# Last batch's attention product in split float16, with all engine orders rewritten

## The reference, cut to what matters

```python
def _xattn(teacher_logits, teacher_features, Wq, bq, Wk, bk):
    query = einsum('bnc,dc->bnd', teacher_features, Wq) + bq      # features: (4, 512, 256), d = 128
    key = einsum('bnc,dc->bnd', teacher_features, Wk) + bk
    attention = softmax(einsum('bnd,bmd->bnm', query, key), axis=-1)
    return einsum('bln,bmn->blm', teacher_logits, attention)      # (4, 512, 512)

x = x + _xattn(layernorm(x), ctx_1024, Wq, bq, Wk, bk)            # x: (4, 512, 512)
x = x + _ffn(layernorm(x), gate_w, up_w, down_w)
```

## Time and profile before

| | us |
|---|---|
| median of 3 runs | 609.17 |
| lowest, highest | 608.98, 626.26 |
| the profiled execution's own time | 610.21 |
| its span in the profile | 608.4 |
| TensorE busy in the span | 596.0 (98%) |
| VectorE busy | 484.3 (80%) |
| ScalarE busy | 316.6 (52%) |

### The profile page before, as it was taken

How to read it: one execution, slowest core, us unless ns; L and a number is a source line. 1 busy time by engine, 2 the same in 40 slices (tenths; PEclk the granted TensorE clock), 3 DMA queues, 4 the chain that set the end, 5 groups by cost and what they waited for, 6 DMA issues and landing times.

```text
span 608.4 us, 7111 instructions
## 1 busy us (share of the span) xinstructions
PE 596.0 (98%) x2619; PEld 274.1 (45%) x2619; DVE 484.3 (80%) x455; ACT 316.6 (52%) x466; POOL 54.4 (9%) x60
## 2 busy tenths in 40 slices
PE   8998999999999899999999999999999999999998
PEld 3444444444444344444444444444444444444446
DVE  4999879997998998879848598857499699575850
ACT  3999999955444425355735436554031522432441
POOL 0020101310200301001000111010000000000010
PEclk9998999999999999999999999999999999999999
DMA  8968789979677408957786788956432105755393
GB/s 319 392 142 247 234 177 295 229 176 287 136 218 170 112 2 258 219 132 178 193 144 129 160 201 222 172 121 122 86 67 40 17 1 86 106 102 87 70 164 62
DMA packets 148212, 95.43 MB, mean 157 GB/s; under 512 B 134353, under 2 KB 134737, under 8 KB 142801
## 3 DMA queue, kind: packets, MB, share of 16 engines
q1 hardware_dynamic: 142704, 66.92, 46.4%
q0 software_dynamic: 5472, 28.05, 20.1%
HBM read 26.81 MB, written 10.49 MB: 61 GB/s over the span
## 4 chain that ended last, share of the span: by engine, by line
PE 63%; DVE 11%; DMA 10%; ACT 8%; issue 7%; SPq 1%; DVEq 0%; ACTq 0%; POOLq 0%
PE bank L759 26%; PE bank L771 17%; PE bank L774 9%; PE bank L743 5%; DMA W<-hT 3%; PE bank L720 2%; DMA h<-hT 2%; PE bank L728 2%; ACT mag L958 2%; DMA gu_lo<-hT 1%; PE bank L789 1%; DVE h L1680 1%; DVE h L1692 1%; DVE h L1496 1%; DVE hscale L1675 1%
## 5 line engine op out<-in xcount | busy, mean ns | idle before, releaser
L759 PE MATMUL bank<-gu_hi,xT 128*128 128x512 f16 x1024 | 245.1, 379 | 3.9 <-ACT silu L1126 3.8
L759 PEld LDWEIGHTS bank<-gu_hi,xT 128*128 128x128 f16 x1024 | 99.4, 98 | 127.0 <-issue 6.1
L759 PE MATMUL bank<-gu_lo,xT 128*128 128x512 f16 x512 | 131.4, 379 | 0.0
L771 PE MATMUL bank<-dn,hT 128*128 128x512 f16 x480 | 106.1, 379 | 1.2 <-ACT silu L1126 1.2
L1126 ACT ACTIVATE silu<-bank,unscale 128x512 f32<-128x512 f32 x64 | 43.0, 679 | 75.3 <-PE bank L759 34.7
L759 PEld LDWEIGHTS bank<-gu_lo,xT 128*128 128x128 f16 x512 | 50.1, 98 | 60.4
L1663 DVE SCALAR_TENSOR_TENSOR h<-bank,unscale,silu 128x512 f32<-128x512 f32 x64 | 47.1, 747 | 34.4 <-ACT silu L1126 19.4
L771 PEld LDWEIGHTS bank<-dn,hT 128*128 128x128 f16 x480 | 46.9, 98 | 58.1 <-ACT silu L1126 1.7
L1496 DVE SCALAR_TENSOR_TENSOR h<-mag,h 128x2048 f32<-128x2048 bf16 x18 | 41.2, 2289 | 32.0 <-ACT mag L958 32.0
L743 PE MATMUL bank<-dn,h 128*128 128x512 f32 x128 | 57.8, 607 | 1.9 <-ACT dn L1043 1.9
L958 ACT ACTIVATE mag<-h 128x2048 bf16<-128x2048 f32 x18 | 34.3, 1905 | 40.0 <-DVE h L1680 30.5
(11 more groups left out here) (134 smaller groups left out, 569.9 us busy)
## 6 DMA issues: line engine op xcount, KB each, us to landing
W<-hT POOLq DMA_DIRECT2D x12, 1024.0 KB, 6.0
W<-in_units SPq DMA_DIRECT2D x11, 1024.0 KB, 5.8
h<-W POOLq DMA_DIRECT2D x7, 1024.0 KB, 5.9
h<-in_xcols SPq DMA_DIRECT2D x4, 1024.0 KB, 11.1
out_y<-y POOLq DMA_DIRECT2D x12, 256.0 KB, 4.5
h<-in_xrows SPq DMA_DIRECT2D x2, 1024.0 KB, 12.6
h<-hT POOLq DMA_DIRECT2D x2, 1024.0 KB, 6.2
out_y<-h SPq DMA_DIRECT2D x2, 1024.0 KB, 5.1
```

What stands on the lines that cost most here:

```text
L759: last = pe.matmul(bank[:, :], xT[:, b % 2, part, k, :], w[:, c, g, j * 512:(j + 1) * 512], start=(j == 0 and not low), stop=(j == HT - 1 ...
L771: pe.matmul(bank[:, :], hT[:, r % 2, 0, k, :], dn[:, w, k, :], start=(k == 0 and w == 0), stop=False)
```

## The change

For the batches in `split`, which is batch 3 alone, `attend` is done with float16 factors. x is multiplied by one scale `xup` for the whole batch, found from the largest of (mean squared plus sum of squares) over the rows: `bound` on VectorE, an all-reduce over the partitions on GpSimd (`bound_max`), a logarithm and an exponential on ScalarE (`x_scale`). The scaled x is split in two float16 parts, `xt_hi` on ScalarE and `xt_lo` on VectorE; the turned probabilities, times 2^14, are split by `take_probs` on ScalarE and `probs_lo` on VectorE. Each tile then has twelve float16 matmuls in place of four float32 ones. `x_unscale` makes the factor with which `add_attended` takes the scales out again. `center` of batch 2 now also waits for the attended tiles of all batches, since the parts of x lie where it writes.

```diff
 def attend(b, lt):
-    for j in range(HT):
-        last = pe.matmul(bank[:, :], xTf[b % 2][:, j, lt * P:(lt + 1) * P], AT[:, j, :],
-                         start=(j == 0), stop=(j == HT - 1))
+    if b in split:
+        pe.wait_ge(xlo_ready, split.index(b) + 1)
+        for n, (p, q) in enumerate(((0, 0), (0, 1), (1, 0))):
+            for j in range(HT):
+                last = pe.matmul(bank[:, :], xT_parts[b][:, p, j, lt * P:(lt + 1) * P], AT_parts[:, q, j, :],
+                                 start=(n == 0 and j == 0), stop=(n == 2 and j == HT - 1))
...
+def xt_hi(b):                        # ScalarE
+    act.wait_ge(xdown_ready, n + 1)
+    act.wait_ge(probs_turned, LT * (4 - b))
+    nc.scalar.activation(xT_parts[b][:, 0, :, :], xTf[b % 2], ACT.Copy, scale=xup[:, n:n + 1])
...
+def xt_lo(b):                        # VectorE
+    dve.wait_ge(xhi_ready, n + 1)
+    dve.scalar_tensor_tensor(xT_parts[b][:, 1, :, :], xTf[b % 2], xup[:, n:n + 1], xT_parts[b][:, 0, :, :],
+                             ALU.mult, ALU.subtract)
...
+def probs_lo(b, nt):                 # VectorE
+    dve.scalar_tensor_tensor(AT_parts[:, 1, :, cols], bank_of(f"t{b}.{nt}"), A_SCALE,
+                             AT_parts[:, 0, :, cols], ALU.mult, ALU.subtract)
...
 TensorE's order, from the last tile of batch 2 on
             attend(2, 3)
+            product(2, 0)
+            product(1, 0)
             turn_probs(3, 0)
+            product(3, 0)
             turn_probs(3, 1)
+            product(0, 0)
             turn_probs(3, 2)
-            product(3, 0)
-            product(1, 0)
-            product(2, 0)
+            product(0, 1)
             turn_probs(3, 3)
-            product(0, 0)
+            product(3, 1)
+            product(2, 1)
             attend(3, 0)
             attend(3, 1)
             attend(3, 2)
+            attend(3, 3)
             product(1, 1)
-            product(3, 1)
-            attend(3, 3)
-            product(0, 1)
-            product(2, 1)
...
 SyncE's order, the first loads
+            load_consts()
             load_slice(0)
             load_ctx(0)
-            load_consts()
+            load_rows(0)
             load_half(0)
             load_rest(0)
```

More of the change, by code:

```diff
@@ L89, in xattn_ffn @@
     slice_size = 256
+    split = (3,)
     parked = (5, 6)
@@ L238, in xattn_ffn @@
         xmean_ready = sem("xmean_ready")
-        xstats_ready = [sem(f"xstats{b}_ready") for b in range(B)]
         ymean_ready = sem("ymean_ready")
@@ L741, in attend @@
                 pe.wait_ge(at_ready, LT * (b + 1))
-                for j in range(HT):
-                    last = pe.matmul(bank[:, :], xTf[b % 2][:, j, lt * P:(lt + 1) * P], AT[:, j, :],
-                                     start=(j == 0), stop=(j == HT - 1))
+                if b in split:
[4 more added lines that the diff above has]
+                                             start=(n == 0 and j == 0), stop=(n == 2 and j == HT - 1))
+                else:
+                    for j in range(HT):
+                        last = pe.matmul(bank[:, :], xTf[b % 2][:, j, lt * P:(lt + 1) * P], AT[:, j, :],
+                                         start=(j == 0), stop=(j == HT - 1))
                 last.then_inc(attended, 1)
@@ L1541, in add_attended @@
                 row = slice(LT * b + lt, LT * b + lt + 1)
[L1542 removed]
+                if b in split:
+                    dve.wait_ge(xatt_ready, split.index(b) + 1)
+                each = xatt if b in split else xrstd
+                dve.scalar_tensor_tensor(rows, bank_of(f"a{b}.{lt}")[:, :], each[:, row], rows, ALU.mult, ALU.add,
                                          accum_out=ysum[:, row]).then_inc(x1_ready, 1)
@@ L1824, in _ @@
+            unit_reduce(8)
+            rows_round(2)
+            rows_dequant(2)
+            unit_largest(8)
+            hidden_of(5, 2)
             hidden_of(6, 2)
+            unit_scale(8)
+            hidden_of(0, 2)
             unit_reduce(9)
-            unit_largest(8)
+            attended_means(3)
+            hidden_of(2, 2)
+            unit_power(8)
+            unit_round(8)
+            unit_reduce(10)
+            hidden_of(4, 2)
             hidden_of(3, 2)
+            unit_dequant(8)
@@ new lines, in _ @@
+            hidden_scale(9)
+            hidden_dequant(8)
+            hidden_lo(7)
+            hidden_of(12, 1)
+            hidden_scale(10)
+            hidden_of(12, 3)
+            hidden_lo(8)
+            hidden_round(9)
+            hidden_of(14, 0)
+            hidden_dequant(9)
+            hidden_of(14, 2)
+            hidden_round(10)
+            hidden_scale(11)
+            hidden_round(11)
+            hidden_dequant(10)
+            hidden_of(12, 2)
+            hidden_lo(9)
```

980 lines of the change are left out of this document (500 added, 480 removed), and 10 rows, old and new, of the table products.

## The result

The changed kernel takes 623.9 us (median of 4 runs, 622.2 to 624.4) against 609.1 of the kernel before. The ratio is 1.023, with a 95% interval of 1.021 to 1.025: slower, where 604.5 with a range of 600 to 611 was forecast. The ratio compares fast runs alone: one of the four runs of the kernel before was slow (626.3 us). The profiled execution took 622.2 us, its span is 620.4, 12.0 longer than before.

What follows compares the result with a forecast made beforehand. TensorE was taken as the bound, busy 596.0 of 608.4 us. Parts 1 to 6 summed as -3.4 - 0.3 + 0 + 1.3 + 0 - 2.5 = -4.9 us, giving a median of 604.5, 80% range 600.0 to 611.0.

Steps and rivals of the forecast that it cites:

- Part 1: Batch 3's four attended tiles: 48 float16 matmuls replace 32 float32 records on TensorE, -3.4 us.
- Part 2: TensorE's wait and clock drop before batch 1's first tile stay: 0.3 us gain, between 1.5 gain and 2 loss.
- Part 3: New first loads, 1 MB of x ahead of unit 0: 0 charged, 3 us loss at most; first product at 86-88 us.
- part 5: Added work beside TensorE, 6.2 us on VectorE, covered by 2.4 us until product(5, 1)'s bank: 0 charged.
- Part 4: Second pair of units wanted sooner, near 109 to 111 us: 1.3 us of waiting charged, within 0 and 5.
- Rival B: VectorE becomes the bound between 100 and 145 us: slower, 614.4 us, up to 617; chance 0.14.
- Part 6: TensorE's six waits for silu, 5.0 us, halve with fewer tight banks: -2.5 us, between -5 and +2.5.

Runs made afterwards that it cites:

- e13: Changed kernel with second_norm(3) earlier, SyncE loads and first loads put back, early ScalarE order of e7 and small edits on ScalarE and VectorE: 610.1 us, ratio 1.002.
- e6: Kernel before with the split alone, in its old order, tables and banks, x scaled by a constant 32: 631.1 us, ratio 1.035.
- e8: Kernel before with the SyncE loads of unit 3 and the third columns issued ahead of the wait for unit 1's rest: 610.8 us, ratio 1.002.
- e15: Kernel before with add_out(0) and second_norm(3) behind hidden_rest(3) on GpSimd, as the change had it: 616.5 us, ratio 1.012.
- e2: Changed kernel with the SyncE loads of unit 3 and batch 2's columns put back behind unit 1's turned high part: 619.2 us, ratio 1.016.
- e9: Changed kernel with one GpSimd line moved, second_norm(3) ahead of hidden_rest(3) and add_out(0): 615.0 us, ratio 1.008.
- e5: The changed kernel itself, unchanged, measured again on another chip: 624.8 us, ratio 1.025.
- e7: Changed kernel with e2's loads, silu_of(11,2) and two down-product copies ahead of hidden-row steps, and ScalarE's copies of turned probabilities earlier: 621.2 us, ratio 1.020.
- e10: e7 with second_norm(3) moved as in e9: 617.3 us, ratio 1.011.
- e11: e10 with the first loads as in e4 and, on VectorE, hidden_of(5,1) ahead of unit_dequant(6): 614.8 us, ratio 1.008.
- e16: e10 without its reordering around 384 us: 612.1 us, ratio 1.006.
- e17: e13 with two ScalarE moves: batch 2's turned-probability copies ahead of attended_variances(0,1) and unit_hi(2), rows_hi(0) ahead of row_variances(2,0): 609.7 us, ratio 1.001.
- e12: Kernel before with the split alone as in e6, its VectorE and ScalarE steps at other places: 616.7 us, ratio 1.011.
- e1: Changed kernel without the split, batch 3's attended tiles in float32 again, new orders kept: 630.9 us, ratio 1.034.
- e3: Changed kernel with silu_of(11,2) on ScalarE ahead of three steps of hidden rows: 620.3 us, ratio 1.016.
- e14: e9 without the split, all attended tiles in float32: 622.0 us, ratio 1.022.
- e4: Changed kernel with SyncE's first loads as before, constants and batch 0's rows behind the first slice and context: 621.7 us, ratio 1.020.

## Why the prediction was wrong

The mechanism failed and not only a size: the forecast took the new places in the queues of SyncE and GpSimd to cost nothing, and there the loss began. Part by part:

**Part 1** holds: 10.5 us in an unbroken row. It is kept, and with the faults of these orders around it the split is worth 7, not 3.4. In e13 nothing of it is seen in the time.

**Part 2** holds in its mechanism and range. "The wait is at least 1.6 us" was 2.56, and the 24 records behind it take 12.24 us as before, so the 0.3 us of gain was a loss of 0.7. But the 1.9 us that it charges to the clock were one profile's: behind the same wait of 1.87 us of the kernel before the records take 10.5 us in e6, e8 and e15.

**Part 3** is where the first half of the error lies. The forecast charged 0 for the start, "Neither is TensorE's wait" (and further up: "start and tail, which the change does not touch"), and expected the first product at 86 to 88. VectorE started at 11.6 us, later than the 10.8 expected, TensorE itself waits for the context (2.7 us, and 1.5 by the clock), and the first product is at 97.1. The start is the smaller part of these 10 us. The larger is in the sentence that ends **part 5**, "SyncE and GpSimd have no new transfers, only other places in their queues". It gives no number to either queue. On SyncE the other place makes the adding DMA of unit 1 take 11.3 us instead of 6.5, in the stretch where ScalarE was known to be full. ScalarE stands 3.6 us for it, and these make the most of TensorE's 4.5 us of wait and 2.6 of clock (e2, e8). What stays of the wait without the loads, 2.4 us in e2, is ScalarE's own longer list. ScalarE's 4.6 us of added work ahead of the first product were counted, but set against idle time of its first 30 us. That idle time lies ahead of the copies TensorE waits for only if the inputs are there.

**The same sentence** hides the second half. On GpSimd the other place is worth about 7.5 us (7.5 of the 9.0 by which the spans of e9 and e5 differ, 7.4 in e15). The forecast said that it would be wrong "if a stretch past 300 us waits for turned hidden rows: there VectorE and ScalarE have idle time, and I count nothing". It does wait there, for a silu. Idle time of an engine over a stretch is no cover for a result that it must have at one point.

**Part 4** was hardly put to the test: the first product of units 2 and 3 follows with no wait for a transpose near 119 us, but the first product of all was 10 us late, and that gave the units time. Where it started at 90 to 93 us (e7, e10, e11, e13, e16, e17), TensorE waited 0.4 to 0.7 us for a turned low part near 115 us. So the wait is real, and 1.3 was too much by half. **Rival B**, the one forecast of a slower kernel (614.4, up to 617), did not come: no wait for VectorE between 100 and 145 us. It is real, though, in the old orders (e12).

**Part 6**: without the one at 384 us the waits for silu fell from 5.0 to 0.5 us, and 2.3 us for VectorE's reads of up banks came instead: -2.2, where -2.5 was forecast. The count of tight banks was a fair guide. It could not show a wait whose cause is three engines away.

With the measured sizes the parts that had a number come to -3.4 + 0.7 + 0 - 2.2 = -4.9 us, just the forecast's sum. That the two agree is chance: part 2 was 1.0 worse than its term and part 6 0.3, and part 4's 1.3 stayed away behind the late first product. What had no number was the start (4.0 us of waits where 1.0 was before, and 1.5 of clock), the wait at 78 us (4.5 + 2.6) and the one at 384 (5.3 + 1.4): 18.3 us, less 0.7 by which the zeros ended sooner. Together that is 12.7 us, where the spans differ by 12.0.

## What to carry to other kernels

When a change rewrites orders, each queue has to be followed, the short ones above all: for every instruction that moved past a DMA on GpSimd or SyncE, write down who reads its result, when, and how much cover was there before. A short operation belongs ahead of a DMA whose input comes late. A wait that only changes its releaser when the waiting instruction is moved has its cause further up: go back from each late engine to the first that stood without being late itself. Test such a cause both ways; that a loss appears when the fault is put into the good kernel (e15) says more than that a bad one gets better, and where it doesn't appear (e8), what the good kernel has is cover.

## What the runs showed of the hardware

GpSimd stands for a long time ahead of a small tensor operation, whatever stands before it. In all 20 profiles each of the three `second_norm` operations (60 in all, about 1 to 3 us long) begins 6.7 us or more after GpSimd's item before it. In 20 of them that item is a reduction over the partitions and not a DMA, and the gap is 6.7 to 7.7 us; behind an adding DMA, where no releaser is shown, it is 6.8 to 8.1. Each reduction that follows such an operation, directly or with one DMA between, begins 5.9 us or more after the item before it (40 of them), while reductions behind DMAs alone, and DMAs behind the operation (350.83 above), can follow at once. Three rows of the changed kernel:

```profile
110.39 0.34 POOL L622 PARTITION_ALL_REDUCE umax<-smax  x1 [3.18 <-DVE smax L1686]
118.11 1.05 POOL L633 TENSOR_TENSOR rstd<-var,mhalf 128x4 f32<-128x4 f32 x1 [7.38 <-issue]
...
163.78 1.34 POOL L622 PARTITION_ALL_REDUCE umax<-smax  x1 [6.41 <-issue]
```

So the 7.5 us ahead of `second_norm(3)` are its own and not the DMA's, and they were there in the kernel before (8.3 us), where they lay in time that nobody needed. What GpSimd does in them no run shows. The start of an item on GpSimd is a rough figure in a trace, but that the result comes late is not: VectorE starts right behind it, at 369.57 us.

Behind an adding DMA the next one comes late in places: `add_out(0)` began 5.2 to 5.8 us after the end of `hidden_rest(3)` in the changed kernel, e9 and e15, with its inputs long there, but in the kernel before 2.1 us after `hidden_rest(2)`, and after the DMA at 365.99 us the next followed within 0.3 us. What makes the difference wasn't tried. The Trainium skill (DMA: Bandwidth & Descriptors, "Anatomy of one DMA — SWDGE (gpsimd) path") puts most of such a DMA's fixed cost of about 2 us into completion and little into its setup. No row here splits that cost; GpSimd's own time for each is 0.9 to 1.2 us.

An adding DMA of 1 MB took 5.8 and 6.5 us (e2 and the kernel before) when one load of 1 MB was issued within the 5 us ahead of it, and 11.1 and 11.3 us with three (e8 and the changed kernel).

The granted clock fell behind idle stretches of TensorE of 1.9, 2.6, 2.7, 4.5 and 5.3 us, but not each time. The 24 records of attended tiles behind the wait of 2.6 us near 55 us take 12.2 us in the profile of the changed kernel and in those of e1, e3, e9 and e14, and 10.5 us, without a drop, in those of e2, e4 and e5. e5 is the same kernel as the changed one, and the wait was 2.57 and 2.56 us. Behind the 1.87 us of the kernel before it is the same: 12.2 us in its own profile, 10.5 in those of e6, e8 and e15, of which e15 has the same orders up to there. So one profile of such a place is 1.7 us unsure, whatever the order.
